# Flamingo block with a two-expert feed-forward: slot 0 gathered in whole rows, expert 1 loaded in part before the routing, other step orders

## The reference

```python
q1 = fake_quant(layernorm(x)); q2 = fake_quant(ctx_4096)          # 8 bits
x = x + tanh(g_xattn[0]) * (q1 @ q2)                              # per batch
h = layernorm(x)
_, top_idx = top_k(h @ W_gate + b_gate, 2)                        # 8 experts
y_all = relu(einsum('bsd,edh->bseh', h, W_e) + b_e)
x = x + tanh(g_ffn[0]) * take_along_axis(y_all, top_idx[..., None], axis=2).mean(axis=2)
```

## Time and profile before

| | |
|---|---|
| median of 3 runs | 373.47 us |
| the profiled execution, its own time | 372.75 us |
| its span, first to last instruction | 371.0 us |
| mean granted TensorE clock | 0.934 |
| busy: TensorE, VectorE, ScalarE, GpSimd | 86%, 68%, 35%, 53% |
| chain that ended last | TensorE 37%, VectorE 25%, issue 11%, GpSimd 11%, DMA 6% |

### The profile page before, as it was taken

One profiled execution on the slowest core, in us unless ns is written; L12 is line 12 of the kernel. 1 busy time (PEld: TensorE's weight loads), 2 busy tenths in 40 slices (PEclk: granted clock), 3 DMA queues, 4 the chain that ended last, 5 costly groups with the idle time before them and its releaser, 6 DMA issues.

```text
span 371.0 us, 6691 instructions
## 1 busy us (share of the span) xinstructions
PE 320.1 (86%) x1602; PEld 241.0 (65%) x1612; DVE 253.9 (68%) x348; ACT 129.2 (35%) x109; POOL 198.1 (53%) x208
## 2 busy tenths in 40 slices
PE   4669887999668798599997999999999999999950
PEld 1224364577543586488885888887888888788840
DVE  3898997878975719639887593587553955695430
ACT  3865876453100263108361711360116310811100
POOL 4552451300426860467782686576566856766661
PEclk9699999999758899699999899999999999999985
DMA  6999385412262595957999799579656896714553
GB/s 233 414 408 391 144 335 233 170 57 85 112 259 72 188 406 215 324 112 168 368 342 408 182 307 324 116 189 409 171 113 160 255 357 137 175 46 99 119 121 57
DMA packets 20012, 81.46 MB, mean 220 GB/s; under 512 B 4256, under 2 KB 4256, under 8 KB 15904
## 3 DMA queue, kind: packets, MB, share of 16 engines
q1 hardware_dynamic: 12272, 57.71, 40.6%
q0 software_dynamic: 7584, 23.60, 27.8%
q10 hardware_dynamic: 144, 0.01, 0.0%
HBM read 62.43 MB, written 18.87 MB: 219 GB/s over the span
## 4 chain that ended last, share of the span: by engine, by line
PE 37%; DVE 25%; issue 11%; POOL 11%; DMA 6%; POOLq 3%; ACT 3%; DVEq 2%; ACTq 0%
PE ps L1222 30%; POOL y_rows L458 7%; DVE w_lo L835 5%; DMA y_rows<-y_scratch,gidx 4%; DVE st L695 4%; PE ps L1028 3%; POOLq L287 2%; POOL gidx L454 2%; DVE xt L759 2%; DMA par<-in_small_dram 2%; DVEq L287 1%; ACT w_hi L630 1%; PE ps_s L1080 1%; DVE onehot L820 1%; DVE res L990 1%
## 5 line engine op out<-in xcount | busy, mean ns | idle before, releaser
L458 POOL DMA_INDIRECT y_rows<-y_scratch,gidx x88 | 110.8, 1259 | 37.7 <-issue 19.8
L1222 PE MATMUL ps<-w_hi,yT_hi 128*128 x320 | 101.2, 398 | 13.4 <-DVE yT_lo L829 13.0
L1222 PE MATMUL ps<-w_hi,yT_lo 128*128 x320 | 100.9, 397 | 0.0
L1222 PE MATMUL ps<-w_lo,yT_hi 128*128 x320 | 100.6, 396 | 0.0
L616 ACT ACTIVATE yT_hi<-ps_y 128x1024 fp32r<-128x1024 f32 x21 | 21.5, 1025 | 168.7 <-DVE ps_y L958 104.4
L1222 PEld LDWEIGHTS ps<-w_hi,yT_hi 128*128 128x128 f32 x320 | 61.2, 192 | 28.6 <-issue 16.0
L835 DVE TENSOR_TENSOR w_lo<-stage,w_hi 128x2048 f32 (+1 forms) x32 | 71.1, 2274 | 0.1
L1222 PEld LDWEIGHTS ps<-w_hi,yT_lo 128*128 128x128 f32 x320 | 61.6, 192 | 13.1
L1222 PEld LDWEIGHTS ps<-w_lo,yT_hi 128*128 128x128 f32 x320 | 61.2, 191 | 12.9
L486 POOL DMA_INDIRECT out_dram<-res,sidx x20 | 32.6, 1632 | 51.9 <-DVE res L992 34.4
L630 ACT ACTIVATE w_hi<-stage 128x2048 f32 x28 | 51.9, 1909 | 13.5 <-DMA stage<-in_L_ffn_W_e_dram 13.5
(11 more groups left out here) (161 smaller groups left out, 259.4 us busy)
## 6 DMA issues: line engine op xcount, KB each, us to landing
stage<-in_L_ffn_W_e_dram SPq DMA_DIRECT2D x32, 1024.0 KB, 7.3
stage<-in_ctx_dram SPq DMA_DIRECT2D x16, 512.0 KB, 11.4
xt<-in_x_dram SPq DMA_DIRECT2D x8, 512.0 KB, 11.1
y_scratch<-y SPq DMA_DIRECT2D x8, 512.0 KB, 3.4
bias<-in_L_ffn_b_e_dram SPq DMA_DIRECT2D x8, 512.0 KB, 4.6
out_dram<-xt SPq DMA_DIRECT2D x6, 512.0 KB, 3.0
y_rows<-y_scratch,gidx POOLq DMA_INDIRECT x88
out_dram<-xt POOLq DMA_DIRECT2D x2, 512.0 KB, 7.8
```

Of the source, the lines that this page charges most:

```text
L458: pool.indirect_dma_start(out=y_rows[q][:, b * QD:(b + 1) * QD], out_offset=None, in_=y_quarters[:, :], in_offset=bass.IndirectOffsetOnAxi ...
L1222: last = pe.matmul(ps[q][:, h * 512:(h + 1) * 512], lhs[q][:, k, :], w[:, bass.ds(woff + k * D + h * 512, 512)], start=(k == 0 and lhs is ...
```

## The change

The weights are read as they are given: partition p holds the rows 8p to 8p + 7, and `turn_rows` reads every eighth element (a step of 32 bytes) of the gathered quarter. Slot 0's rows come by one indirect DMA of 128 whole rows of 4 KB through `idx`, and TensorE transposes them. Two chunks of expert 1 are loaded between the stores of y(5) and y(6), the other two when the last chunks of expert 0 are split. VectorE turns the rows of slot s + 2 at the end of step s, after relu; it writes `idx` earlier. GpSimd issues two of the four quarter gathers ahead of the scatter and two behind it. ScalarE waits for the table after the first `evacuate_hi`, not before. There are fewer filler matmuls.

```diff
-    w_t = W_e.rearrange("e p k h -> p e k h")
+    w_t = W_e.rearrange("e (p k) h -> p e k h", p=P)
...
+            def load_w1(c):
+                sp.dma_start(stage[:, CK * c:CK * (c + 1), :], w_t[:, 1, CK * c:CK * (c + 1), :]).then_inc(s_w[c], 16)
...
-            for i in range(TPB, NT):
-                store_y(i)
+            store_y(4)
+            store_y(5)
+            for c in range(2):
+                sp.wait_ge(s_lo, c + 1)
+                load_w1(c)
+            store_y(6)
+            store_y(7)
...
-            for q in range(2):
-                sp.wait_ge(s_g[q], 16 * NQ)
-            with sp.Fori(1, E) as n:
+            for c in range(2, NCH):
+                sp.wait_ge(s_lo, c + 1)
+                load_w1(c)
+            with sp.Fori(2, E) as n:
...
-            def gather(slot, q, step):
+            def pick_rows(slot, q, step):
...
-                for b in range(NQ):
+            def gather_quarters(q, first, end):
+                for b in range(first, end):
                     pool.indirect_dma_start(out=y_rows[q][:, b * QD:(b + 1) * QD], out_offset=None, in_=y_quarters[:, :],
...
+            pool.wait_ge(s_idx, 1)
+            pool.indirect_dma_start(out=y_rows[0][:, :], out_offset=None, in_=y_dram[:, :],
+                                    in_offset=bass.IndirectOffsetOnAxis(ap=idx[:, 0:1], axis=0)).then_inc(s_g[0], 16)
             pool.wait_ge(s_qidx, 1)
-            for b in range(NQ):
-                pool.indirect_dma_start(out=y_rows[0][:, b * QD:(b + 1) * QD], out_offset=None, in_=y_quarters[:, :],
-                                        in_offset=bass.IndirectOffsetOnAxis(ap=qidx[:, 0, b:b + 1], axis=0)
-                                        ).then_inc(s_g[0], 16)
             pool.wait_ge(s_col, 1)
-            gather(1, 1, 1)
+            pick_rows(1, 1, 1)
+            gather_quarters(1, 0, NQ)
             pool.wait_ge(s_tp, 1)
-            gather(2, 0, 2)
+            pick_rows(2, 0, 2)
+            gather_quarters(0, 0, NQ)
...
             def step(slot, q, turn):
                 pool.wait_ge(s_tp, slot + 2)
-                gather(slot + 3, 1 - q, slot * 2 + 3)
+                pick_rows(slot + 3, 1 - q, slot * 2 + 3)
+                gather_quarters(1 - q, 0, NQ // 2)
...
                                         in_=res[q][:, :], in_offset=None, compute_op=ALU.add).then_inc(s_sc, 16)
+                gather_quarters(1 - q, NQ // 2, NQ)
...
-            act.wait_ge(s_tab, 1)
             act.wait_ge(s_tp, 1)
             evacuate_hi(0, 0)
+            act.wait_ge(s_tab, 1)
...
-            link(dve.tensor_scalar(cnt8[:, :], ps_c[:, NT * E:(NT + 1) * E], 1.0 / P, 0.494, ALU.mult, ALU.add))
-
-            link(dve.tensor_scalar(count[:, 0:E], cnt8[:, :], 1.0, None, ALU.max))
             dve.wait_ge(s_abs, 1)
             dve.tensor_scalar(idx[:, :], tok_abs[:, :], 1.0, -1.0, ALU.max, ALU.add).then_inc(s_idx, 1)
+            link(dve.tensor_scalar(cnt8[:, :], ps_c[:, NT * E:(NT + 1) * E], 1.0 / P, 0.494, ALU.mult, ALU.add))
+
+            link(dve.tensor_scalar(count[:, 0:E], cnt8[:, :], 1.0, None, ALU.max))
...
                 dve.transpose(ps_y[:, :, :].rearrange("p k (b r) -> p k b r", b=NQ),
-                              y_rows[q][:, :].rearrange("p (b k r) -> p k b r", b=NQ, k=KT)).then_inc(s_tp, 1)
-
-            turn_rows(0, 1)
+                              y_rows[q][:, :].rearrange("p (b c k) -> p k b c", b=NQ, k=KT)).then_inc(s_tp, 1)
...
                 evacuate_lo(1 - q)
-                dve.wait_ge(s_el, slot + 2)
-                turn_rows(q, turn + 2)
                 with dve.If(nxt > 0):
...
                                   ALU.max, ALU.mult).then_inc(s_post, 1)
+                dve.wait_ge(s_el, slot + 2)
+                turn_rows(q, turn + 1 + q)
...
-            keep_clock(4, ps[0][:, 512:1024])
+            keep_clock(2, ps[0][:, 512:1024])
...
-            keep_clock(30, ps[0][:, 512:1024])
+            keep_clock(14, ps[0][:, 512:1024])
+            pe.wait_ge(s_g[0], 16)
+            for k in range(KT):
+                last = pe.transpose(ps_y[:, k, :], y_rows[0][:, :].rearrange("m (p k) -> m k p", k=KT)[:, k, :],
+                                    ident_f[:, :])
+            last.then_inc(s_tp, 1)
+            keep_clock(6, ps[0][:, 512:1024])
...
-    w = _np.asarray(inputs["L0_ffn_W_e"])
-    n_e, n_d, n_h = w.shape
-    given["L0_ffn_W_e"] = w.reshape(n_e, 4, n_d // 128, 32, n_h).transpose(0, 1, 3, 2, 4).reshape(n_e, 128, n_d // 128, n_h)
```

More of the change, by code:

```diff
@@ L362, in _ @@
                                  ).then_inc(s_w[c], 16)
[L363 to L371, removed]
+                sp.wait_ge(s_post, entry(sp, BAS - 1, n, MAX_SLOTS, lo=1))
+                settle(sp)
+                for q in range(2):
+                    with sp.If((n & 1) == q):
+                        sp.dma_start(bias[:, q * D:(q + 1) * D],
+                                     b_e[bass.ds(n, 1), :].rearrange("a d -> (a d)").partition_broadcast(P)
+                                     ).then_inc(s_bias[q], 16)
                 sp.nop()
@@ L492, in _ @@
             pool.wait_ge(s_sc, n * 16 + 32)
-            pool.wait_ge(s_g[0], ((n + 4) >> 1) * (16 * NQ))
+            pool.wait_ge(s_g[0], ((n + 2) >> 1) * (16 * NQ) + 16)
             pool.wait_ge(s_g[1], ((n + 3) >> 1) * (16 * NQ))
@@ L915, in _ @@
             count, base_, rest = cnt[:, 0, :], cnt[:, 1, :], cnt[:, 2, :]
+            dve.wait_ge(s_abs, 1)
+            dve.tensor_scalar(idx[:, :], tok_abs[:, :], 1.0, -1.0, ALU.max, ALU.add).then_inc(s_idx, 1)
             link(dve.tensor_scalar(cnt8[:, :], ps_c[:, NT * E:(NT + 1) * E], 1.0 / P, 0.494, ALU.mult, ALU.add))
             link(dve.tensor_scalar(count[:, 0:E], cnt8[:, :], 1.0, None, ALU.max))
-            dve.wait_ge(s_abs, 1)
-            dve.tensor_scalar(idx[:, :], tok_abs[:, :], 1.0, -1.0, ALU.max, ALU.add).then_inc(s_idx, 1)
             dve.wait_ge(s_spread, 1)
@@ L952, in _, with turn_rows @@
             dve.wait_ge(s_tab, 1)
-            def turn_rows(q, n_gathers):
-                dve.wait_ge(s_g[q], n_gathers * (16 * NQ))
+            def turn_rows(q, quartered):
+                dve.wait_ge(s_g[q], quartered * (16 * NQ) + (16 if q == 0 else 0))
                 settle(dve)
                 dve.transpose(ps_y[:, :, :].rearrange("p k (b r) -> p k b r", b=NQ),
-                              y_rows[q][:, :].rearrange("p (b k r) -> p k b r", b=NQ, k=KT)).then_inc(s_tp, 1)
-            turn_rows(0, 1)
+                              y_rows[q][:, :].rearrange("p (b c k) -> p k b c", b=NQ, k=KT)).then_inc(s_tp, 1)
             dve.wait_ge(s_eh, 1)
```

## The result

The changed kernel takes 384.88 us (median of 4 runs, 383.48 to 385.59), the kernel before on the same chip 374.22 (4 runs, 369.62 to 375.26): ratio 1.0326, 95% interval 1.0242 to 1.0409, so slower. The forecast was 379 in a range to 384.

A forecast was written before the change was run, and what follows sets the result against it. Matmuls bound TensorE from slot 7, 10.97 us a slot. 9.9 gained by slot 2's end, 9.3 lost by slot 8's, then slots, stalls and clock to 365.9; end 377.2, plus 1.75: 379 us, range 359 to 384.

The forecast's parts named there:

- The turn: VectorE's turn of 1024 elements, now reading in steps of 8: 2.26 us each, against 1.26 before.
- Rival 1: A stepped read on VectorE costs nothing, the turn stays 1.26 us: time 360, 3.5% faster; chance 0.33.
- The stall of a lone splitting step: TensorE's wait for yT_lo when one step splits weights: 2T - 2.18, T being the turn's time; 2.34 us at 2.26.
- M(8): End of slot 8's matmuls on TensorE, forecast at 236.1 us.
- M(19): End of slot 19's matmuls on TensorE, forecast at 365.9 us.
- Rival 2: TensorE's idles before slots 11, 15 and 18 each cost the whole 1.65 us of lower clock: 382, 2.2% slower; chance 0.19.
- Slot 0: Start of slot 0's matmuls on TensorE: at 118.3 us instead of 123.22, 4.9 earlier.
- Turn of slot 1: 116.75 + 5.54 = 122.3: VectorE's turn at the start: comes 5.54 us after slot 0's yT_lo ends at 116.75, so at 122.3.
- M(2): End of slot 2's matmuls on TensorE: at 156.5 us against 166.44, 9.9 gained.
- 7.8 to the end of the span: The tail: from the last scatter's start to the end of the span 7.8 us, taken from the earlier profile.
- The early half of expert 1 is worth 0 alone: Loading half of expert 1's weights early gains 0, as ScalarE had the chunks before VectorE, which waited for the gather.
- The gathers behind the scatter: Two of each step's quarter gathers, issued later on GpSimd: charged 0, because slots without a split have slack.

The follow-up runs named there:

- The second run: The changed kernel with slot 0's old path, the old row order of the weights and the plain turn, still late: 366.15 us, ratio 0.9866 to the kernel before.
- the first run: The changed kernel with slot 0's old path (four quarter gathers, turn on VectorE, 30 fillers), turn still stepped: 380.07 us, ratio 1.024 to the kernel before.

## Why the prediction was wrong

**The turn: right.** Forecast 2.26, measured 2.12. The second run takes it away and shows that it is the main cause of the slower time: 3.8% in the late place. The rule of the Trainium skill on cachelines ("Advanced Engine Details and Errata", "SBUF Cachelines") held for this read: 2.12 against 1.25 us for the same 1024 elements. Rival 1 fell with it.

**The stall of a lone splitting step: right at two slots of four.** 2T - 2.18 gives 2.06 for T = 2.12; slots 8 and 18 waited 2.05 and 2.00, slots 11 and 15 only 1.44; why these are shorter is open. Forecast from M(8) to M(19) 129.8, measured 127.7; three clocks of 0.7 were charged, and one of 1.6 was lost.

**Rival 2, the clock:** half right. An idle of 2.0 cost the lower clock at slots 8 and 18, one of 1.44 at slots 11 and 15 did not. But 2.0 us isn't a sure limit: with all gathers ahead of the scatter, slot 8 took only 10.98 behind an idle of 2.02, and slot 11 took 12.58 behind one of 2.23.

**Slot 0:** forecast 118.3, measured 120.32, of which 1.66 is that tok_abs came later (110.76 against 109.10). Other traces had it at 108.9 to 111.4 (leaving out the two with small early gathers), the kernel before with a late extra gather at 111.36, so it is taken as no part of the change. The landing, 4.31, was forecast as 4.0.

**"Turn of slot 1: 116.75 + 5.54 = 122.3" failed.** The prediction took VectorE for the bound and the gather for landed. With tok_abs's 1.66 it would be 124.0; it was 127.47, since the four issues could only start at 116.41 and the last, beside the splits, took 2.77. In the earlier trace rows slot 1's gather had been hidden. This is what the earlier slot 0 ran into, and the first run shows that nothing of its lead is left at slot 5. M(2) was 161.35 instead of 156.5; some 3 us of that hang on the slow issue, which started only 0.34 us too late.

**"7.8 to the end of the span" failed, and it is the term that put the time out of the range.** M(19) was forecast at 365.9 and measured at 366.57, the errors before it cancelling: M(2) 4.9 late, the stretch behind it 4.2 shorter than the forecast. From M(19) to the end 11.3 were forecast and 16.0 measured, 4.1 of it the closing DRAIN, which I had taken over from a kernel without the 4 KB gather. With that term right the forecast would have been 383. That it would have been so near is luck in part, as M(19) was right only because the errors cancelled.

**"The early half of expert 1 is worth 0 alone" failed.** It is worth some 1.1 to 1.7% (the experiments move all four chunks, not the half alone). The argument that VectorE waited for the gather was right, but it let the gather land as late as before, after the 7.90 of the earlier trace rows, and beside two chunks of weights instead of four it landed after 4.9. In the late place no turn waits there, and VectorE's splits gain by having their chunks. The gathers behind the scatter, charged 0, cost 0 beside the stepped turn and perhaps 0.7% beside the plain one.

So the parts, as ratios to the kernel before: expert 1's loads 0.989, with the plain turn late and the gathers ahead 0.979. The stepped turn takes the late place from a gain of 1% to a loss of 3%, and the lead of slot 0, which the 4 KB gather brings, is gone by slot 5 beside the late stepped turn, while the gather adds 4 us in the DRAIN.

## What to carry to other kernels

A change of layout that saves a step once and makes a repeated one slower is priced by the repeated one, and by its place: 0.87 us a turn cost 1.4 to 3.5% ahead of the splits, in the kernel before, and 3.8% or 14 us between relu and yT_lo, where in the splitting steps it lay on the chain that the next slot waits for. A step that is brought forward is worth what the next one in line allows: ask for that one's transfer, too, when it is issued and beside what. Here a third of a microsecond decided whether an issue on GpSimd was held by an operation of VectorE, and 3 us hung on it. And the tail of the program is to be priced anew when the kind of DMA on a queue changes, even if the last microseconds are untouched.

## What was not expected of the hardware

- GpSimd's closing DRAIN takes 5.26 to 5.43 us in kernels with one indirect gather of 4 KB a row ahead of the quarter gathers, and 1.10 to 1.26 without it, with it at the end, or with three more gathers issued after the last scatter had landed.
- The issue of an indirect gather on GpSimd takes about 0.95 us. Started within one of VectorE's splits, a TENSOR_TENSOR that reads two SBUF tiles, it took 1.83 us or more in 341 of 344 cases, and 329 of them ended 0.8 to 0.9 us after that split. Started beside VectorE's other operations, or 0.02 us ahead of the split, it was not held: at most 1.45 in 1386 cases.
- An idle of TensorE of 1.44 us left the clock alone; after one of 2.0 us the slot behind it took 1.6 to 1.7 us more at slots 8 and 18, and nothing more in one other run (2.02).
- Three small gathers on GpSimd during attention, where it seemed idle, went with an attention stage longer by 1.4 to 3.9 us than in the other traces (tok_abs at 112.84 against 108.9 to 111.4); the cause is open.
